# A decoder layer on one core: three stages written out instead of looped

## The reference

```python
x = x + delta_net(layernorm(x))            # 16 key heads, 2 value heads each, width 128
x = x + cross_attention(layernorm(x), ctx) # 16 heads of width 16, 512 x 512 scores per batch
x = x + W2 @ fwht(silu(W1 h) * (W3 h))     # h = layernorm(x), hidden width 2048

# the recurrence of the first block, one step per token
Sk    = k_t . state
delta = (v_t - Sk) * beta_t
state = state * decay_t + k_t delta
o     = q_t . state
```

## Time and profile before

| | |
|---|---|
| median of three runs | 4286.8 us |
| the profiled execution | 4285.89 us |
| its span, first to last instruction | 4284.1 us |
| mean granted clock of TensorE | 0.969 |
| PE busy | 3929.7 us (92%) |
| DVE busy | 2938.0 us (69%) |
| ACT busy | 2431.1 us (57%) |
| POOL busy | 630.9 us (15%) |

### The profile page before, as it was taken

One profiled execution on the slowest core, in us unless ns is written; L12 is line 12 of the kernel. 1 busy time (PEld: TensorE's weight loads), 2 busy tenths in 40 slices (PEclk: granted clock), 3 DMA queues, 4 the chain that ended last, 5 costly groups with the idle time before them and its releaser, 6 DMA issues. The chain is left out here.

```text
span 4284.1 us, 75444 instructions
## 1 busy us (share of the span) xinstructions
PE 3929.7 (92%) x26288; PEld 2918.3 (68%) x26288; DVE 2938.0 (69%) x5022; ACT 2431.1 (57%) x4813; POOL 630.9 (15%) x585
## 2 busy tenths in 40 slices
PE   3899999999999999999999999995798989699998
PEld 2677777777777777777777777773444444488886
DVE  3788888887887878888888888884555555422222
ACT  2677677776676767767677767762345454411111
POOL 0000000000000000000000000002346554400110
PEclk8999999999999999999999999997899999899999
DMA  2010111010100101011010110002656665210001
GB/s 77 16 43 26 34 36 34 26 39 20 38 31 26 43 17 44 26 34 36 16 44 26 34 36 33 27 16 58 106 99 108 105 113 90 81 43 10 20 15 40
DMA packets 156748, 188.82 MB, mean 44 GB/s; under 512 B 13340, under 2 KB 97052, under 8 KB 156348
## 3 DMA queue, kind: packets, MB, share of 16 engines
q1 hardware_dynamic: 153916, 182.62, 18.1%
q10 hardware_dynamic: 2432, 1.05, 0.2%
HBM read 151.31 MB, written 30.15 MB: 42 GB/s over the span
## 5 line engine op out<-in xcount | busy, mean ns | idle before, releaser
L406 PE MATMUL pj<-xh,w_hi 128*128 128x512 f32 x1536 | 684.1, 445 | 16.8 <-DVE w_lo L745 16.5
L406 PE MATMUL pj<-xh,w_lo 128*128 128x512 f32 x1536 | 607.4, 395 | 0.0
L406 PE MATMUL pj<-xl,w_hi 128*128 128x512 f32 x1536 | 601.0, 391 | 0.0
L1056 POOL TENSOR_TENSOR silu_z<-silu_z,exp_z 128x512 f32<-128x512 f32 x128 | 185.2, 1468 | 2643.6 <-ACT exp_z L632 2643.6
L1614 DVE TENSOR_REDUCE row_max<-s 128x1 f32<-128x512 f32 x512 | 340.8, 686 | 281.6 <-PE s L1360 278.4
L1546 ACT ACTIVATE probs<-s 128x512 f32<-128x512 f32 x512 | 293.1, 595 | 325.2 <-PE s L1384 321.1
L406 PEld LDWEIGHTS pj<-xh,w_hi 128*128 128x128 f32 x1536 | 291.0, 189 | 65.6 <-DVE w_lo L745 17.0
L406 PEld LDWEIGHTS pj<-xh,w_lo 128*128 128x128 f32 x1536 | 288.7, 188 | 66.0
L406 PEld LDWEIGHTS pj<-xl,w_hi 128*128 128x128 f32 x1536 | 292.2, 190 | 50.1 <-issue 14.8
L1384 PE MATMUL s<-q_stack,k_stack 128*128 128x512 f32 x512 | 251.9, 494 | 72.6 <-DMA q_stack<-row_maxima 68.3
L811 DVE SCALAR_TENSOR_TENSOR conv_v<-conv_in,conv_w_section,conv_v 128x512 f32<-128x512 f32 x384 | 287.8, 750 | 10.7 <-ACT conv_v L615 1.6
(11 more groups left out here) (257 smaller groups left out, 9925.5 us busy)
## 6 DMA issues: line engine op xcount, KB each, us to landing
w_raw<-in_w_in SPq DMA_DIRECT2D x128, 256.0 KB, 6.2
decays<-decay_by_head SPq DMA_DIRECT2D x64, 512.0 KB, 3.8
decays<-decay_by_head SPq DMA_DIRECT2D x64, 256.0 KB, 5.1
q_stack<-qk_parts SPq DMA_DIRECT2D x128, 128.0 KB
k_stack<-qk_parts SPq DMA_DIRECT2D x128, 128.0 KB
f_raw<-in_f_w SPq DMA_DIRECT2D x32, 256.0 KB, 2.6
x_all<-in_x SPq DMA_DIRECT2D x4, 1024.0 KB, 9.9
source<-in_ctx SPq DMA_DIRECT2D x8, 512.0 KB
```

What stands on the lines that cost most here:

```text
L406: mm = pe.matmul(pj[j % 2][:, :], a[:, j, k * P:(k + 1) * P], b[:, k, bp * WIN:(bp + 1) * WIN], start=(n == 0), stop=(n == 3 * KT - 1))
L1056: pool.tensor_tensor(sz[p][:, :], sz[p][:, :], ez[p][:, :], ALU.mult).then_inc(E["sz"].sem, 1)
```

## The change

The device loops of the three stages are replaced by Python loops, so that every round is written out. All calls keep their arguments and their order; the rounds' numbers are now constants, and so are the values waited for.

```diff
             prologue(eng)
-            head(0, True, False)
-            with eng.Fori(1, HK - 1) as hk:
-                head(hk, False, False)
-            head(HK - 1, False, True)
+            for hk in range(HK):
+                head(hk, hk == 0, hk == HK - 1)
             epilogue(eng, Section(HK - 1, NSEC - 1), HK - 1)
...
             start(eng)
-            for f in range(2):
-                unit(eng, f, 0, f, True, True)
-            with eng.Fori(1, BATCH - 1) as b:
-                for f in range(2):
-                    unit(eng, b * 2 + f, b, f, True, True)
-            for f in range(2):
-                unit(eng, (BATCH - 1) * 2 + f, BATCH - 1, f, f == 0, False)
+            for u in range(UNITS):
+                unit(eng, u, u // 2, u % 2, u < UNITS - 1, u < UNITS - 2)
...
-            with sp.Fori(1, GROUPS) as g:
+            for g in range(1, GROUPS):
                 load(g, False)
...
-            slices(0)
-            with act.Fori(1, GROUPS * NW) as r:
+            for r in range(GROUPS * NW):
                 slices(r)
...
-            group(0)
-            with dve.Fori(1, GROUPS) as g:
+            for g in range(GROUPS):
                 group(g)
```

## The result

| | before | after |
|---|---|---|
| median | 4286.69 us (4 runs) | 4251.23 us (4 runs, 4249.68 to 4253.82) |
| profiled execution | 4285.89 us | 4249.73 us |
| its span | 4284.1 us | 4247.9 us |
| mean granted clock of TensorE | 0.969 | 0.967 |

The ratio after to before is 0.9924, with a 95% interval from 0.9911 to 0.9936. The forecast was 4251 us.

A forecast was written before the change was run, and what follows sets the result against it. PE bounds the delta stage, where 13 jumps back stall the instruction streams. Removing them gains 36.1 us, the other stages 0: span 4284.1 to 4248.0, plus 1.8 outside and 0.9 for the median, 4251 us; range 4243 to 4263.

The forecast's parts named there:

- D: Delta stage: time between DVE's L792 of head 1 and of head 15, 2456.16 us before, forecast 2420.0.
- The straight head as a yardstick: Delta stage: sections of straight heads 0 and 15 give 172.86 us per head, expected for all 14 looped heads.
- Registers: Delta stage loop: register instructions cost next to nothing, head 1 being 0.10 us longer in section 0 than head 15.
- The jump's two parts: Delta stage: each jump costs 2.29 us in the section ending over it and 0.68 us in the next.
- the bounds of 14.9 and 8.9 us: Most that could be gained in cross-attention (5 jumps) and the last stage (3 jumps), at 2.97 us each.
- rival 2: Delta stage: the 0.68 us behind each jump stays, so the gain is 29.8 us, time 4257; 7 in 100.
- PE's 2.94 us: Delta stage: PE's delay per jump, from 4.20 us between heads in straight code to 7.14 over the jump.
- Cross-attention at 0: Cross-attention: removing 5 jumps per engine gains 0, their cost lying under the row maxima's transfer through memory.
- Last stage at 0: Last stage: PE is already straight and ACT, DVE and SP wait for it, so unlooping them gains 0.
- Code late in the cross stage: Cross-attention: exposed code fetches lose 48 us, time 4299, 3 in 100; milder form 4257 to 4275, 6 in 100.
- A gain in the other stages: Cross-attention and last stage gain up to 14.9 and 8.9 us, time 4227, or 4243 for a third; 6 in 100.
- Straight code fetched as badly: Delta stage: straight heads in a long stream are fetched as badly as after a jump, 4287 us; 3 in 100.

The follow-up runs named there:

- one_round_loops: The changed kernel with each of heads 1 to 14 of the delta stage in a loop of one round, no jump back: 4246.04 us, kernel before 4282.43.
- two_heads: The changed kernel with the delta stage looped, two heads per round, 6 jumps back in place of 13: 4266.03 us, kernel before 4282.43.
- dve_act_straight: The changed kernel with the delta stage looped on PE alone, straight on DVE and ACT: 4281.80 us, kernel before 4281.03.
- pe_straight: The changed kernel with the delta stage looped on DVE and ACT, straight on PE alone: 4265.75 us, kernel before 4281.03.
- rest_only: The changed kernel with the delta stage's loop put back, the other two stages written out: 4283.34 us, kernel before 4281.03.
- rotated_cross: The changed kernel with cross-attention looped again, its 4 jumps moved to step 16 of an even unit: 4250.13 us, kernel before 4282.37.
- short_jumps: The changed kernel with a two-round loop over one fulfilled wait added after each head but the last, on each engine: 4250.60 us, kernel before 4282.43.
- all_straight: The changed kernel with the remaining loops, of layer norms and row statistics, also written out: 4244.86 us, kernel before 4282.37.
- long_cross: The changed kernel with cross-attention looped, two batches per round, 2 jumps at step 16 of an odd unit: 4254.98 us, kernel before 4287.37.

## Why the prediction was right

**What bounds, and the clock.** The 13 waits on "issue" were the right thing to start from, and the distance between L792 rows was the right measure: D was forecast at 2420.0 us and is 2420.63. That the time, forecast at 4251, is 4251.23 is luck in its last microseconds: the cross stage of this profiled run was 3.57 us shorter by a short batch, the stretches before and after the delta stage 3.25 longer, and other kernels scatter by as much. Counting only the idle time that DVE shows would have given 30.4 of the 35.5 us.

**The straight head as a yardstick.** 172.86 us per head, from heads 0 and 15, holds for all 14: they take 172.83 to 173.03.

**Registers and jumps.** Registers were put at 0.10 us per head; one_round_loops makes it 0.03, while in two_heads section 0 without a jump before it takes 43.04 to 43.07 us, the prediction's 43.05. The jump's two parts, 2.29 and 0.68 us, were both real, and the second is PE's (dve_act_straight keeps it, pe_straight loses most of it). Their sizes came from the first jump alone. Over all 13, the section over the jump takes 44.51 us on average (43.84 to 44.98), 1.96 more than the 42.55 of straight code, and the one behind it 43.73, 0.78 more than 42.95: 2.74 in all, not 2.97. The forecast was not touched by this, since it was added up from straight heads; the bounds of 14.9 and 8.9 us and the 29.8 of rival 2 were. The prediction spoke of PE's 2.94 us as the jump's price. The runs refine that: PE's own jump is worth 2.37 us, and ACT's and DVE's, when PE has none, 1.17 and 0.92. They overlap, and together come to 2.5 to 2.7.

**Cross-attention at 0.** The number held (rest_only), the reason did not: "whatever the jump costs lies under that transfer" falls with rotated_cross. A round of one batch can be jumped back over in the open at no cost; with two batches in a round PE stops. The evidence that I had, equal waits with and without a jump, fitted both readings. The 2 packets of the earlier trace rows in five looped batches would have told them apart: nothing was being fetched again. So the right number here had a mechanism that was wrong for this loop, and the bound of 14.9 us had nothing behind it. The comparison inside a unit took odd units alone; in even ones the registers add 0.16 us between steps 3 and 20 (21.16 to 21.20 before, 21.00 to 21.02 after), and that too ends in the wait for the row maxima.

**Last stage at 0.** Right by rest_only. DVE's loop there has 3 rounds and so 2 jumps back, not the 3 of the bound: 5.9 us, not 8.9. Whether its jumps are covered by PE's work or free by themselves was not tried.

**The rivals.** Code late in the cross stage: more packets came, 14 for 3 on q8 from 3110 to 3520 us, and the waits show 0.3 us on "issue" once, on ACT. A part of the debt that stays: section 0 is 42.95 us, none stays. A gain in the other stages: none in rest_only. Straight code fetched as badly: no wait on "issue" of the jumps' kind is left.

The rule on taken branches of the Trainium skill ("Runtime: NRT & Kernel Launch", "Instruction fetch mechanics") is borne out, with the condition that matters here: only jumps out of the code that is held cost something, 2.7 us before and nothing in short_jumps, and the packets of the instruction queues go with it. The same place says that kernels prefer full unrolling where possible. By rest_only and all_straight, writing out the short loops brings nothing.

## What to carry to other kernels

Look for waits on "issue" that come exactly once per round of a loop on the device, and if the kernel has a few rounds in straight code, measure their difference from the looped ones at one fixed instruction; that is the whole gain, debts to later work included. The packets of the instruction queues tell beforehand which loops can pay: 3 in 410 us in a loop whose body stays, and more than straight code takes in one whose body is fetched again. Write out loops with long bodies, on every engine that takes part (PE alone gave 15.3 us of some 35, DVE and ACT alone nothing); short loops and the registers of their indices can stay. A cost that doesn't show in one place needs an experiment before it is called hidden: here it wasn't there. And a stop that shows is not yet time lost: the two of long_cross went into a wait that followed.

## What the runs showed of the hardware

- A jump back costs by how long the loop's body is, because a long body is fetched again in every round. On PE a body of 293 listing rows (867 records, 55 KB at 64 bytes a record) is not fetched again (3 packets on q8 in 410 us) and costs nothing; one of 586 (about 1734 records, 111 KB) is (21 packets) and stops PE for 2.3 to 2.6 us. On ACT a body of 202 rows (238 records) and on DVE one of 172 (189 records) stay; after bodies of 280 rows (380 records) and 342 (458 records) ACT stops for 2.0 to 2.3 us on average and DVE for 2.2 to 2.4. Where between them the cost begins was not tried.
- The delta stage takes 145 packets on q8 and 74 on q14 in straight code, and 179 and 139 with its loop. In straight code no wait on "issue" there is over 0.3 us.
- Two heads in a body, twice the length, cost no more per jump than one: the section over the jump takes 44.50 us on average, and 44.51 with one head.
- The stops of three engines lie side by side: 2.37, 1.17 and 0.92 us of the stage for one alone, 2.5 to 2.7 for all.
- Loops of two rounds over one wait cost 0.18 us for 14 jumps on each of three engines.
- A stop of PE of 2.3 to 2.6 us in the middle of a unit of cross-attention did not lengthen that stage: PE's idle time before the next even unit, else 4.5 to 6.4 us for the row maxima, was 0.73 and 0.81.
- Open: the batches of 82.4 to 82.9 us in cross-attention in place of 85.3, which move the span by up to 7.4 us from one profiled run to the next; and ACT's and DVE's own part in the stop of long_cross.
